# Performer attention: features by two groups of 64 contraction rows, context by swapped operands in four groups of 32 columns

## The chip, the cores and the metric

The kernel runs on one core of one Trainium2 chip. The metric is the device time of one execution in microseconds (us); lower is better. A comparison takes the median of several runs.

## The reference, cut to what matters

A batch of 8 sequences of 1024 rows by 256 columns goes through four layers: causal attention, a 4-bit-quantised MLP, Performer attention with an MLP, and a dequantised MLP. The change touches the third alone, and of it the attention:

```
q, k, v = split(video @ W.T + b)                  # 16 heads of 16 columns
def features(x, is_query):                        # proj is 64 x 16
    xp   = (x * 16**-0.25) @ proj.T               # 64 features for each head and row
    diag = sum(x**2) * 0.5 * 16**-0.5
    stab = max(xp over features)      if is_query # per row and head
           max(xp over features, rows) otherwise  # per head
    return 64**-0.5 * (exp(xp - diag - stab) + 1e-4)
qp, kp = features(q, True), features(k, False)
ctx = kp.T @ v                                    # per head 64 x 16, and kp.T @ 1 for the denominator
out = (qp @ ctx) / (qp @ sum(kp))
attn = out @ Wo.T + bo
```

## The kernel before, in words

Everything is float32 in memory. A product that needs full precision at high speed is written as three matmuls of split operands (`product`, lines 267 to 271): high part times high part, high times low, low times high. Other matmuls (transposes, context, output, half squares) take float32 operands as they are.

The Performer attention (`performer_attention`, from line 1072) works batch by batch on 8 tiles of 128 rows. For each batch there is a *front* (normalised rows are transposed, `t`; k is projected, `k`; v is projected, `v`; half squares of k, `s`; features of k for the 8 tiles, `f`), a *tail* (q is projected, the maximum over k is spread, then for the 8 tiles the features of q, the exponentials, the transposes of q's features and the context), and an *out* part (output product, division, transposes and the Wo product for the 8 tiles). `merged(b, b + 1)` interleaves the out part of one batch with the front of the next, in nine slots by the hand-written list `FRONT`; `tail(b)` runs between. All engines follow the same order, each with its own instruction list, and semaphores tie them.

- `features(i)` (line 1486): for tile i and each half c of the 256 columns of q or k, one `product` with a stationary operand of 128 rows by 128 columns (the transposed q or k) and 512 moving columns. The moving operand `proj` is block-diagonal: 8 heads of 16 rows, 64 columns each. So 6 matmuls of 128x512 for a call. It is called 8 times for k (in `front`, line 1525) and 8 times for q (in `tail`, line 1580).
- The q features of a tile go to VectorE (maximum, line 1377; add the half squares, line 1379; subtract, line 1383), to ScalarE (exponential, line 1463), back to TensorE (8 transposes, line 1586), and to ScalarE (copy, line 1460). The k features get their shift subtracted by GpSimd (line 1230) and their exponential from ScalarE (line 1457).
- The context (line 1599): for each tile 8 matmuls, one for two heads: stationary are 128 columns of k's exponentials, moving are 34 columns of v (16 columns and a column of ones for each head). Half of each 128x34 result belongs to no head pair and is not read. Before the first tile one matmul (line 1595) puts in the constant's share, with 272 moving columns `v_sum`.
- At the end of the tail VectorE copies the two useful halves into `ctx_pair` (line 1396), and TensorE's next output product (line 1544) waits for that.

In the tail TensorE's order for step i is: features of tile i, transposes of tile i - 2, context of tile i - 1. It has 10 steps.

Of the kernel before, what the change touches and what calls it, by code (L numbers as in the profile page):

```python
# [1040 lines left out]

class PerformerRaw:
# [29 lines left out]
def performer_attention(core, dram, attn_dram, raw, mlp_raw):  # L1072
# [7 lines left out]
    with ExitStack() as ctx:  # L1080
# [17 lines left out]
        with ExitStack() as prep:  # L1098
# [3 lines left out]
            @block.gpsimd  # L1102
            def _(pool):
                pool.memset(keps[:, :], KEPS).then_inc(made, 1)
                pool.memset(ones[:, :], 1.0).then_inc(made, 1)

                pool.memset(square_sum[:, :, :], 0.0).then_inc(made, 1)
                pool.wait_ge(made, 3)
                for c in range(KD):
                    pool.memset(square_sum[:, c, c * HC:(c + 1) * HC], 0.5 * DH ** -0.5).then_inc(made, 1)  # L1110
                pool.wait_ge(made, 3 + KD)
                for c in range(KD):
                    part_c = square_sum[:, c, c * HC:(c + 1) * HC]
                    pool.affine_select(out=part_c, in_=part_c, compare_op=ALU.is_ge, fill=0.0, base=0,
                                       pattern=[[-DH, HC]], channel_multiplier=1).then_inc(made, 1)
                    pool.wait_ge(made, 4 + KD + 2 * c)
                    pool.affine_select(out=part_c, in_=part_c, compare_op=ALU.is_ge, fill=0.0, base=DH - 1,
                                       pattern=[[DH, HC]], channel_multiplier=-1).then_inc(made, 1)
                pool.wait_ge(made, 3 + 3 * KD)
# [30 lines left out]
        v_sum = sbuf("p_v_sum", [P, HEADS * VW])  # L1150
# [10 lines left out]
        qfT = kf[:, :, :].rearrange("p t (k q) -> p t k q", k=PAIRS)  # L1161
        ctx_pair = sbuf("p_ctx_pair", [P, PAIRS, 2 * VW])
# [25 lines left out]
        ctx_done, ctx_copied = sem("p_ctx_done"), sem("p_ctx_copied")  # L1188
# [22 lines left out]
        @block.gpsimd  # L1211
        def _(pool):
            def tile_of_v(i):
                return v[:, i].rearrange("p h w -> p (h w)")

            with pool.Fori(0, B) as b:
                pool.wait_ge(var_ready, b + 1)
                pool.tensor_tensor(rstd[:, bass.ds(b * TB, TB)], var_eps[:, :], core.minus_half[:, :],
                                   ALU.pow).then_inc(rstd_ready, 1)
                pool.wait_ge(v_ready, b * 4 + 4)  # L1220
                for i in range(1, TB):
                    if i > 1:
                        pool.wait_ge(v_summed, b * (TB - 1) + i - 1)
                    pool.tensor_tensor(v_sum[:, :], v_sum[:, :] if i > 1 else tile_of_v(0), tile_of_v(i),
                                       ALU.add).then_inc(v_summed, 1)
# [34 lines left out]
        def _(dve):  # L1260
# [87 lines left out]
            def tail(b, last):  # L1348
# [44 lines left out]
                dve.wait_ge(ctx_done, b + 1)  # L1393
                for r in range(2):
                    rows = slice(r * M, (r + 1) * M)
                    dve.tensor_copy(ctx_pair[rows, :, r * VW:(r + 1) * VW],
                                    ps_a[rows, 0:PAIRS * 2 * VW].rearrange("p (k w) -> p k w", k=PAIRS)
                                    [:, :, r * VW:(r + 1) * VW]).then_inc(ctx_copied, 1)
# [69 lines left out]
        def _(pe):  # L1468
# [7 lines left out]

            def half_squares(b, ps, k, half):
# [80 lines left out]
            def tail(b, last):  # L1558
# [15 lines left out]
                for i in range(TB + 2):  # L1574
# [13 lines left out]
                    if 1 <= i <= TB:  # L1588
# [15 lines left out]

            pe.wait_ge(ones_set, 2)
            run(tail, merged)(pe)
# [517 lines left out]
def host_layout(inputs):  # L2124
# [11 lines left out]
    for n in "qkvo":  # L2136
        a[f"p_w{n}T"] = inputs[f"L1_attn_W{n}"].T
    for n in "kq":
        a[f"p_b{n}"] = columns(inputs[f"L1_attn_b{n}"])
# [43 lines left out]
```

## Time and profile before

| | |
|---|---|
| time, median of 3 runs | 2728.48 us (2715.63 to 2732.13) |
| the profiled execution's own time | 2712.57 us |
| its span, first to last instruction | 2710.9 us |
| mean granted TensorE clock | 0.952 |
| TensorE matmuls busy | 2439.4 us (90%), 16012 records |
| VectorE, ScalarE, GpSimd busy | 1960.4, 1196.5, 733.1 us |

The span is the time of one execution between its first and last instruction on the engines. Busy time of TensorE counts a matmul from its start to its modelled end, and neighbours overlap, so the distance from start to start is read rather than the duration. A granted clock of 1.00 is 2.4 GHz, 0.50 is 1.2 GHz.

### The profile page before, as it was taken

What the parts mean: (1) busy time and instruction counts of PE and PEld (TensorE: products, weight loads), DVE (VectorE), ACT (ScalarE), POOL (GpSimd) and SP (SyncE); (2) the same over time, 40 slices, a digit from 0 to 9 for tenths busy, and PEclk for the clock granted to TensorE, in tenths of its full rate; (3) what the DMA queues carried; (4) which work ended last, traced back from release to release, by engine and by line L of the source; (5) the groups of instructions that cost most, each with busy time, mean ns of one, the idle gap of its engine ahead of it and who ended that gap; (6) DMA issues with size and microseconds to landing.
All of it is one profiled execution on the core that took longest, in us unless ns stands there. A gap on an engine that the chain in (4) does not pass through costs nothing. (4 is left out here: it accounts for less than half of the span.)

```text
span 2710.9 us, 44219 instructions
## 1 busy us (share of the span) xinstructions
PE 2439.4 (90%) x16012; PEld 2226.7 (82%) x16012; DVE 1960.4 (72%) x3617; ACT 1196.5 (44%) x1864; POOL 733.1 (27%) x452
## 2 busy tenths in 40 slices
PE   7999996889998969999999999958888888799999
PEld 6888885888888868898898899847777777699998
DVE  5666675899999966566566656648999998866664
ACT  4444543343344325445456445523333333444444
POOL 1111111444444433123212312214344442211110
PEclk9999998899999989999999999968999989899999
DMA  5000000000000000000000000020000010100000
GB/s 168 0 0 0 0 0 19 1 1 0 0 0 0 1 16 1 16 8 8 15 12 4 15 15 8 9 67 24 17 24 15 15 39 1 41 17 23 23 23 32
DMA packets 43114, 45.94 MB, mean 17 GB/s; under 512 B 2976, under 2 KB 42016, under 8 KB 42784
## 3 DMA queue, kind: packets, MB, share of 16 engines
q1 hardware_dynamic: 43040, 44.95, 5.3%
q8 instruction: 47, 0.77, 0.1%
q14 instruction: 27, 0.22, 0.0%
HBM read 28.16 MB, written 16.78 MB: 17 GB/s over the span
## 5 line engine op out<-in xcount | busy, mean ns | idle before, releaser
L1738 ACT ACTIVATE m_a<-m_ps_wide,m_b 128x512 f32<-128x512 f32 x128 | 88.4, 691 | 286.4 <-PE m_ps_wide L271 198.6
L1706 PE MATMUL m_ps_z<-m_w_hi,m_a_hi 128*128 128x256 f32 x512 | 152.5, 298 | 53.9 <-DVE m_a_lo L1778 53.8
L1738 ACT ACTIVATE d_a<-d_ps_wide,d_b 128x512 f32<-128x512 f32 x128 | 88.3, 690 | 190.4 <-PE d_ps_wide L271 188.4
L1778 DVE TENSOR_TENSOR d_a_lo<-d_a,d_a_hi 128x512 fp32r<-128x512 f32 x128 | 86.8, 690 | 110.7 <-ACT d_a_hi L1742 109.7
L1230 POOL TENSOR_TENSOR p_kf<-p_kf,p_k_shift 128x1024 f32<-128x1024 f32 x64 | 119.4, 1903 | 155.5 <-DVE p_k_shift L1364 155.5
L1706 PEld LDWEIGHTS m_ps_z<-m_w_hi,m_a_hi 128*128 128x128 f32 x512 | 102.4, 200 | 68.6 <-DVE m_a_lo L1778 63.5
L1706 PE MATMUL m_ps_z<-m_w_lo,m_a_hi 128*128 128x256 f32 x512 | 149.5, 292 | 0.0
L1706 PE MATMUL m_ps_z<-m_w_hi,m_a_lo 128*128 128x256 f32 x512 | 149.2, 291 | 0.0
L1706 PE MATMUL d_ps_z<-d_w_hi,d_a_lo 128*128 128x256 f32 x512 | 145.4, 284 | 0.0
L1706 PE MATMUL d_ps_z<-d_w_lo,d_a_hi 128*128 128x256 f32 x512 | 145.0, 283 | 0.0
L1706 PE MATMUL d_ps_z<-d_w_hi,d_a_hi 128*128 128x256 f32 x512 | 143.9, 281 | 0.3 <-DVE d_a_lo L1778 0.3
L269 PE MATMUL f_ps_gate<-f_gate_w_hi,f_n_T_hi 128*128 128x352 f32 x256 | 93.6, 366 | 39.6 <-ACT f_silu L942 39.6
L1313 DVE TENSOR_REDUCE p_kmax<-p_kf 128x16 f32<-128x1024 f32 x64 | 78.1, 1220 | 65.4 <-ACT p_kf L1429 65.0
L194 POOL TENSOR_TENSOR f_h_q<-f_h_q,f_h_scale 128x1408 f32<-128x1408 f32 x32 | 83.2, 2599 | 155.5 <-DVE f_h_q L191 155.5
L1544 PE MATMUL p_ps_a<-p_ctx_pair,p_kf 128*128 128x34 f32 x1024 | 123.6, 277 | 0.0
L1544 PEld LDWEIGHTS p_ps_a<-p_ctx_pair,p_kf 128*128 128x128 f32 x1024 | 122.7, 196 | 0.4
L1599 PEld LDWEIGHTS p_ps_a<-p_v,p_kf 128*128 128x128 f32 x1024 | 120.2, 192 | 0.8
L1599 PE MATMUL p_ps_a<-p_v,p_kf 128*128 128x34 f32 x1024 | 119.8, 272 | 0.0
L269 PE MATMUL m_ps_wide<-m_h_hi,m_w_hi 128*128 128x512 f32 x256 | 109.0, 426 | 3.8 <-DVE m_h_lo L1771 3.7
L1937 DVE SCALAR_TENSOR_TENSOR m_o<-m_o,m_o_mean,m_g 128x256 f32<-128x256 f32 x64 | 111.9, 1807 | 0.0
L269 PE MATMUL p_ps_feat<-p_proj_hi,p_kqT_hi 128*128 128x512 f32 x256 | 111.7, 436 | 0.0
L1463 ACT ACTIVATE raw_weights<-raw_weights 128x1024 f32<-128x1024 f32 x64 | 67.8, 1060 | 98.5 <-DVE raw_weights L1383 98.5
(342 smaller groups left out, 8707.9 us busy)
## 6 DMA issues: line engine op xcount, KB each, us to landing
residual<-in_x SPq DMA_DIRECT2D x8, 1024.0 KB, 11.8
attn<-p_attn SPq DMA_DIRECT2D x32, 256.0 KB, 2.1
m_attn<-attn SPq DMA_DIRECT2D x16, 512.0 KB, 3.8
out<-residual SPq DMA_DIRECT2D x16, 512.0 KB, 2.9
raw_weights<-in_d_q SPq DMA_DIRECT2D x2, 1024.0 KB, 7.2
d_scale<-in_d_scale SPq DMA_DIRECT2D x2, 1024.0 KB, 6.0
raw_weights<-in_m_w1T SPq DMA_DIRECT2D x1, 1024.0 KB, 4.9
raw_weights<-in_m_w2T SPq DMA_DIRECT2D x1, 1024.0 KB, 9.4
```

What stands on the lines that cost most here:

```text
L194: return pool.tensor_tensor(self.blocked(v), self.blocked(v), self.spread(self.scale[slot][:, :]), ALU.mult)
L269: pe.matmul(out, lhsT[0], rhs[0], start=start, stop=False)
L1230: pool.tensor_tensor(f, f, k_shift[:, i, :].unsqueeze(2).broadcast_to([P, HEADS, M]), ALU.subtract).then_inc(k_shifted, 1)
L1313: small_k.add(dve.tensor_reduce(kmax[:, m, :], kf[:, m, :].rearrange("p (h m) -> p h m", h=HEADS), AX.X, ALU.max))
L1463: act.activation(qf[i % 2][:, :], qf[i % 2][:, :], ACT.Exp).then_inc(q_exp, 1)
L1544: mm = pe.matmul(ps_a[:, k * 2 * VW:(k + 1) * 2 * VW], qfT[:, i, k, :], ctx_pair[:, k, :], start=True, stop=True)
L1599: mm = pe.matmul(ps_a[:, k * 2 * VW:(k + 1) * 2 * VW], kf[:, j, k * P:(k + 1) * P], vt[:, k * 2 * VW:(k + 1) * 2 * VW], start=False, stop= ...
L1706: mm = pe.matmul(z, a, w[:, f, :], start=(f == 0 and k == 0 and j % 2 == 0), stop=(f == FC - 1 and k == 2), skip_group_check=True)
L1738: act.activation(self.a[f % RING][:, :], self.ps_wide[f % 2][:, :], self.func, bias=self.b1[:, f:f + 1])
L1778: dve.tensor_tensor(self.a2[1][:, f, :], self.a[f % RING][:, :], self.a2[0][:, f, :].bitcast(F32), ALU.subtract).then_inc(self.a_lo, 1)
L1937: o_tally.add(dve.scalar_tensor_tensor(o[:, j, :], o[:, j, :], o_moments.mean[:, j:j + 1], g3[:, :], ALU.subtract, ALU.mult))
```

## The change

Features: q and k are laid out so that each half c of their transposed tile holds four heads in rows 0 to 63 and four in rows 64 to 127. Each of the 6 matmuls of 128 rows by 512 columns becomes two of 64 rows by 256 columns, on the two row halves, issued next to each other and written to two different PSUM banks. A call issues 12 matmuls in place of 6. The host permutes the rows of Wq, Wk and their biases; the mask of the half squares follows.

Context: the operands are swapped. For each head a stationary operand of 17 columns (v and the ones) and 64 moving columns (k's exponentials) give a 17x64 result; the four heads issued next to each other go to PSUM partitions 0, 32, 64 and 96. So 16 matmuls for a tile in place of 8, and 16 for the constant's share in place of 1. The result is the transposed context, so at the end of the tail VectorE copies it to SBUF (128x256, over the free `squares` tile), TensorE transposes it with two 128x128 transposes, and VectorE copies the useful halves into `ctx_pair` as before. One matmul at the start of the layer fills the bank, so that rows that no head writes hold numbers.

```diff
             def features(i):
+                hi, lo = kqT
+                n = HR * M
                 for c in range(KD):
-                    mm = product(pe, ps_feat[i % 2][:, c * BANK:(c + 1) * BANK],
-                                 part(kqT, slice(None), c, slice(i * P, (i + 1) * P)), part(proj, slice(None)))
+                    for k, (a, w) in enumerate(((hi, proj[0]), (hi, proj[1]), (lo, proj[0]))):
+                        for r in range(GROUPS):
+                            rows, at = slice(r * RG, (r + 1) * RG), r * BANK + c * n
+                            mm = pe.matmul(ps_feat[i % 2][:, at:at + n], a[rows, c, i * P:(i + 1) * P],
+                                           w[rows, r * n:(r + 1) * n], start=(k == 0), stop=(k == 2))
                 return mm
...
+            def column_order():
+                return [HC * c + 2 * j + r for c in range(KD) for r in range(2) for j in range(CT)]
+
+            def ctx_at(h):
+                j, at = h % HC // 2, (h // HC * 2 + h % 2) * M
+                return ps_a[j * VP:j * VP + VW, at:at + M]
...
-                            pe.matmul(ps_a[:, 0:HEADS * VW], keps[:, :], v_sum[:, :], start=True, stop=False,
-                                      skip_group_check=True)
-                        vt = v[:, j].rearrange("p h w -> p (h w)")
-                        for k in range(PAIRS):
-                            mm = pe.matmul(ps_a[:, k * 2 * VW:(k + 1) * 2 * VW], kf[:, j, k * P:(k + 1) * P],
-                                           vt[:, k * 2 * VW:(k + 1) * 2 * VW], start=False, stop=(j == TB - 1),
-                                           skip_group_check=True)
+                            for h in column_order():
+                                pe.matmul(ctx_at(h), v_sum[:, h, :], keps[:, 0:M], start=(h < HC and h % 2 == 0), stop=False,
+                                          skip_group_check=True)
+                        for h in column_order():
+                            mm = pe.matmul(ctx_at(h), v[:, j, h, :], kf[:, j, h * M:(h + 1) * M], start=False,
+                                           stop=(j == TB - 1), skip_group_check=True)
                         if j == TB - 1:
                             mm.then_inc(ctx_done, 1)
+                pe.wait_ge(ctxT_copied, b + 1)
+                for c in range(KD):
+                    mm = pe.transpose(ps_b[:, c * P:(c + 1) * P], ctxT[:, c * P:(c + 1) * P], ident[:, :])
+                mm.then_inc(ctx_turned, 1)
...
                 dve.wait_ge(ctx_done, b + 1)
+                dve.tensor_copy(ctxT[:, :], ps_a[:, 0:KD * P]).then_inc(ctxT_copied, 1)
+                dve.wait_ge(ctx_turned, b + 1)
```

`RG = 64`, `GROUPS = 2`, `HR = 4`, `VP = 32`, `CT = 4`, `KD = 2`, `M = 64`, `VW = 17`.

## Rows read from the trace of the kernel before

**Rows 1.** Busy time by stretch (PE, PEld, DVE, ACT, POOL, then clock): tail, merged, tail's start.

```profile
1149.50:1189.00 39.50, 38.64 (x277) 35.34 (x276) 30.91 (x52) 24.03 (x25) 16.54 (x9) 0.96 0.00 0
1189.00:1240.00 51.00, 49.91 (x364) 45.93 (x363) 24.08 (x45) 20.55 (x36) 5.35 (x7) 1.00 0.06 21
...
1246.00:1257.00 11.00, 11.00 (x67) 9.84 (x66) 5.29 (x7) 2.57 (x5) 10.87 (x6) 0.84 0.00 0
```

**Rows 2.** Timeline, GpSimd, k's shift in two batches: start us, us, engine, line.

```profile
1149.46 14.92 POOL L1230 TENSOR_TENSOR p_kf<-p_kf,p_k_shift 128x1024 f32<-128x1024 f32 x8 [20.59 <-DVE p_k_shift L1364]
...
1246.13 14.92 POOL L1230 TENSOR_TENSOR p_kf<-p_kf,p_k_shift 128x1024 f32<-128x1024 f32 x8 [20.59 <-DVE p_k_shift L1364]
```

**Rows 3.** Timeline, TensorE: the tail's first feature matmul; one of its 8 steps.

```profile
1153.77 0.48 PE L269 MATMUL p_ps_feat<-p_proj_hi,p_kqT_hi 128*128 128x512 f32 x1
...
1173.56 0.48 PE L269 MATMUL p_ps_feat<-p_proj_hi,p_kqT_hi 128*128 128x512 f32 x1
1173.88 0.39 PE L270 MATMUL p_ps_feat<-p_proj_lo,p_kqT_hi 128*128 128x512 f32 x1
1174.11 0.39 PE L271 MATMUL p_ps_feat<-p_proj_hi,p_kqT_lo 128*128 128x512 f32 x1
...
1175.03 1.03 PE L1586 MATMUL p_ps_turn<-ident,raw_weights 128*128 128x128 f32 x8
1175.90 1.87 PE L1599 MATMUL p_ps_a<-p_v,p_kf 128*128 128x34 f32 x16
1177.61 0.48 PE L269 MATMUL p_ps_feat<-p_proj_hi,p_kqT_hi 128*128 128x512 f32 x1
```

**Rows 4.** Timeline, VectorE in the same tail: first steps, then waits for TensorE.

```profile
1157.10 1.74 DVE L1379 TENSOR_TENSOR p_q_shift<-p_q_shift,p_halfsq_q 128x16 f32<-128x16 f32 x1
...
1161.91 0.65 DVE L1379 TENSOR_TENSOR p_q_shift<-p_q_shift,p_halfsq_q 128x16 f32<-128x16 f32 x1
...
1165.63 0.17 DVE L1379 TENSOR_TENSOR p_q_shift<-p_q_shift,p_halfsq_q 128x16 f32<-128x16 f32 x1
1165.84 1.22 DVE L1383 TENSOR_TENSOR raw_weights<-p_ps_feat,p_q_shift 128x1024 f32<-128x1024 f32 x1
...
1175.23 1.23 DVE L1377 TENSOR_REDUCE p_q_shift<-p_ps_feat 128x16 f32<-128x1024 f32 x1 [0.55 <-PE p_ps_feat L271]
...
1179.28 1.22 DVE L1377 TENSOR_REDUCE p_q_shift<-p_ps_feat 128x16 f32<-128x1024 f32 x1 [0.39 <-PE p_ps_feat L271]
```

**Rows 5.** Timeline, end of the tail and first output product, three engines.

```profile
1186.05 1.06 ACT L1463 ACTIVATE raw_weights<-raw_weights 128x1024 f32<-128x1024 f32 x1 [0.83 <-DVE raw_weights L1383]
...
1188.32 1.07 PE L1586 MATMUL p_ps_turn<-ident,raw_weights 128*128 128x128 f32 x8
1188.52 0.62 DVE L1396 COPY p_ctx_pair<-p_ps_a 64x136 f32<-64x136 f32 x2 [1.86 <-PE p_ps_a L1599]
...
1189.22 1.95 PE L1544 MATMUL p_ps_a<-p_ctx_pair,p_kf 128*128 128x34 f32 x16
...
1191.50 0.42 DVE L1324 TENSOR_TENSOR p_mixed<-p_ps_a,p_inv_den 128x256 f32<-128x256 f32 x1
```

**Rows 6.** Timeline, TensorE in the merged stretch: v's projection (256 columns), a transpose pair.

```profile
1206.70 0.28 PE L270 MATMUL p_ps_feat<-p_wv_lo,p_nT_hi 128*128 128x256 f32 x1
1206.81 0.28 PE L271 MATMUL p_ps_feat<-p_wv_hi,p_nT_lo 128*128 128x256 f32 x1
...
1228.10 0.38 PE L1537 MATMUL p_ps_b<-ident,p_mixed 128*128 128x128 f32 x2
```

**Rows 7.** Timeline, the merged stretch's last slot: the wait there.

```profile
1236.44 0.38 PE L269 MATMUL p_ps_b<-p_wo_hi,p_mixedT_hi 128*128 128x256 f32 x1 [1.09 <-DVE p_mixedT_lo L1337]
```

**Rows 8.** Tile view of `p_ps_a`: two records for each float32 matmul; durations min/median/max in ns.

```profile
L1595 PE MATMUL p_ps_a<-p_v_sum,p_keps x16: 390/392/655, 1062.5 to 1732.8; 128*128 128x272 f32 x16
```

**Rows 9.** Timeline, weight loads: one of 16 columns, and the load after it.

```profile
1243.04 0.09 PEld L1565 LDWEIGHTS p_ps_b<-ident,p_kmax_all 128*16 128x16 f32 x1 [0.47 <-issue]
...
1243.15 0.19 PEld L269 LDWEIGHTS p_ps_feat<-p_nT_hi,p_wq_hi 128*128 128x128 f32 x1
```

More of the change, by code:

```diff
@@ L1039 @@
 HC = HEADS // KD
+RG = 64
+GROUPS, HR = P // RG, RG // DH
+VP = 32
+CT = P // VP
 class PerformerRaw:
@@ L1149, in performer_attention @@
         v = sbuf("p_v", [P, TB, HEADS, VW])
[L1150 removed]
+        v_sum = sbuf("p_v_sum", [P, HEADS, VW])
         halfsq_k, halfsq_q = (sbuf(f"p_halfsq_{e}", [P, TB, HEADS]) for e in "kq")
@@ L1161, in performer_attention @@
         qfT = kf[:, :, :].rearrange("p t (k q) -> p t k q", k=PAIRS)
+        ctxT = squares[:, 0, 0, 0:KD * P]
         ctx_pair = sbuf("p_ctx_pair", [P, PAIRS, 2 * VW])
@@ L1187, in performer_attention @@
         k_shifted, k_exp = sem("p_k_shifted"), sem("p_k_exp")
-        ctx_done, ctx_copied = sem("p_ctx_done"), sem("p_ctx_copied")
+        ctx_done, ctxT_copied = sem("p_ctx_done"), sem("p_ctxT_copied")
+        ctx_turned, ctx_copied = sem("p_ctx_turned"), sem("p_ctx_copied")
         qf_done, q_shifted, q_exp = sem("p_qf_done"), sem("p_q_shifted"), sem("p_q_exp")
@@ L1213, in tile_of_v @@
             def tile_of_v(i):
-                return v[:, i].rearrange("p h w -> p (h w)")
+                return v[:, i, :, :]
             with pool.Fori(0, B) as b:
@@ L1223, in _ @@
                         pool.wait_ge(v_summed, b * (TB - 1) + i - 1)
-                    pool.tensor_tensor(v_sum[:, :], v_sum[:, :] if i > 1 else tile_of_v(0), tile_of_v(i),
-                                       ALU.add).then_inc(v_summed, 1)
+                    so_far = v_sum[:, :, :]
+                    pool.tensor_tensor(so_far, so_far if i > 1 else tile_of_v(0), tile_of_v(i), ALU.add).then_inc(v_summed, 1)
                 pool.wait_ge(k_shift_ready, b + 1)
@@ L1396, in tail @@
                     dve.tensor_copy(ctx_pair[rows, :, r * VW:(r + 1) * VW],
-                                    ps_a[rows, 0:PAIRS * 2 * VW].rearrange("p (k w) -> p k w", k=PAIRS)
-                                    [:, :, r * VW:(r + 1) * VW]).then_inc(ctx_copied, 1)
+                                    ps_b[rows, 0:KD * P].rearrange("p (k w) -> p k w", k=PAIRS)
+                                    [:, :, 0:VW]).then_inc(ctx_copied, 1)
             dve.memset(v[:, :, :, DH:VW], 1.0).then_inc(ones_set, 1)
@@ L1594, in tail @@
                             pe.wait_ge(v_summed, (b + 1) * (TB - 1))
-                            pe.matmul(ps_a[:, 0:HEADS * VW], keps[:, :], v_sum[:, :], start=True, stop=False,
-                                      skip_group_check=True)
-                        vt = v[:, j].rearrange("p h w -> p (h w)")
-                        for k in range(PAIRS):
-                            mm = pe.matmul(ps_a[:, k * 2 * VW:(k + 1) * 2 * VW], kf[:, j, k * P:(k + 1) * P],
-                                           vt[:, k * 2 * VW:(k + 1) * 2 * VW], start=False, stop=(j == TB - 1),
-                                           skip_group_check=True)
+                            for h in column_order():
[4 more added lines that the diff above has]
+                                           stop=(j == TB - 1), skip_group_check=True)
                         if j == TB - 1:
                             mm.then_inc(ctx_done, 1)
+                pe.wait_ge(ctxT_copied, b + 1)
+                for c in range(KD):
+                    mm = pe.transpose(ps_b[:, c * P:(c + 1) * P], ctxT[:, c * P:(c + 1) * P], ident[:, :])
+                mm.then_inc(ctx_turned, 1)
             pe.wait_ge(ones_set, 2)
+            pe.matmul(ps_a[:, 0:PAIRS * 2 * VW], ident[:, :], ctx_pair[:, :, :].rearrange("p k w -> p (k w)"),
+                      start=True, stop=True)
             run(tail, merged)(pe)
@@ L2135, in host_layout, with by_row_group @@
         a[f"f_{n}"] = inputs[f"L0_ffn_w_{n}"]
-    for n in "qkvo":
+    def by_row_group(v):
+        return v.reshape(GROUPS, KD, HR * DH, -1).transpose(1, 0, 2, 3).reshape(v.shape)
+    for n in "vo":
         a[f"p_w{n}T"] = inputs[f"L1_attn_W{n}"].T
     for n in "kq":
-        a[f"p_b{n}"] = columns(inputs[f"L1_attn_b{n}"])
+        a[f"p_w{n}T"] = by_row_group(inputs[f"L1_attn_W{n}"]).T
+        a[f"p_b{n}"] = columns(by_row_group(inputs[f"L1_attn_b{n}"]))
     a["p_bv"] = inputs["L1_attn_bv"]
```

13 lines of the change are left out of this document (7 added, 6 removed).

## The prediction

> **What bounds the kernel now.** I read busy time by stretch first. In a merged stretch TensorE is busy 49.9 of 51 us and VectorE 24.1; in a tail TensorE 38.6 of 39.5, VectorE 30.9, ScalarE 24.0 [rows 1]. The reader should see TensorE full in both and VectorE as the next engine in the tail alone. Two successive batches start k's shift at 1149.46 and 1246.13 [rows 2]: a batch lasts 96.67 us, eight take about 773 us of the 2710.9. What one batch gains or loses counts eight times.
>
> The timeline gives TensorE's work from start to start. A step of the tail is 4.05 us (1173.56 to 1177.61): features 1.47 (six matmuls 0.23 apart, the first 0.32 before the second), transposes 0.87, context 1.71 [rows 3]. In the merged stretch a feature call that follows a like product takes 6 x 0.23 = 1.38. Then VectorE in the same tail: it waits for the features in the later steps, but only 0.55 and 0.39 us (a second 0.39 follows, alike) [rows 4]. So of a step of 4.05 us VectorE itself fills about 3.66 where it also normalises the next batch. Behind TensorE stands an engine that is nearly as slow.
>
> **The change part by part.**
>
> *Features.* Each matmul of 512 columns becomes two of 256 on different rows. 256 columns of this type go out 0.11 to 0.12 apart, take 0.118 [rows 6]. If the two row halves run side by side, six pairs take 6 x 0.118 = 0.71; if they run one after the other, 12 x 0.118 = 1.42, no gain on 1.38. No row of before shows two row groups at work, so these are the two ends. I take side by side, because the two touch neither the same rows nor the same bank and are issued next to each other; the nearest row, though, is the serial one. To the 0.71 I add 0.1 for the first load in front of each call (the 0.32 less 0.23 in [rows 3]) and 0.1 for going back to full height: 0.91 us. A call saves 0.47 in the merged stretch.
>
> The Trainium skill ("TensorE: Matmul & The Clock Gate", Part 3, on packing small matmuls) measured 3.07 times for four row groups of 32, an efficiency of 77%; as an estimate, two groups would then give 1.54 times and a call would be about 1.1 us in place of 0.91. No run here shows it yet.
>
> *k's features in the merged stretch.* TensorE is full there, so a shorter call moves what follows. Five calls lie in slots 5 to 7: 5 x 0.47 = 2.35. In the last slot are three. There TensorE already stands 1.09 us for VectorE's low half of the mixed tile [rows 7]; what f5 saves is added to that wait. Behind it ScalarE's copies and VectorE's maxima follow each other with 1.2 us each, so of the three calls about 0.9 us arrive. Together 3.25, less some 0.15 for new short waits of the same kind in slots 6 and 7: **3.1 us a batch**.
>
> *Context.* A float32 matmul leaves two records (16 for 8 matmuls), and 272 columns last 392 ns, as long as 512 columns of the features [rows 8, 3]: each column costs about two. So 64 columns are like 128; by the line through 0.118 at 256 and 0.23 at 512, one record is 0.0625 us. Now a tile has 16 records at 1.71 / 16 = 0.107, whatever its 34 columns. After, 32 records. Ends: all apart at today's 0.107, 3.42 us; streamed one after another at 0.0625, 2.0; neighbouring heads side by side in different columns, half of that, 1.0. I take 1.5, between the last two: loads of 17 columns are short (0.09 against 0.19 for 128 [rows 9]), but the two records of a head share their columns and can't overlap. The constant's share becomes 16 matmuls too: 1.5 for 0.46 before. It lies in the step in which TensorE waits for VectorE's first subtraction, and the earlier features leave room for it; without that room it costs 1.0 us.
>
> *A step of the tail* is then 0.91 + 0.87 + 1.5 = 3.3 us on TensorE. VectorE needs about 3.66 where it normalises (above) and, by its share of 30.9 us in a whole tail, some 3.3 elsewhere; ScalarE less [rows 1]. So the tail becomes VectorE's, and what it gains is read from VectorE's chain:
> - The first features end earlier: six at 0.23 and more (the clock is at 0.84 here [rows 1]) against pairs, about 0.8 us. VectorE's little addition (line 1379) takes 1.74 and 0.65 us in the first two steps, 0.17 later [rows 4]; each time it ends at a boundary of GpSimd's 1.87 us instructions (14.92 / 8 from 1149.46 [rows 2]: 1158.8, 1162.5). Start 0.8 earlier and the first ends one boundary sooner, at 1156.9, the second at 1160.7, and the third at 1164.4, when GpSimd is done. The third subtraction then starts at 1164.4 instead of 1165.84: 1.5 us gained.
> - The waits for features go: 0.55 + 0.39 + 0.39 = 1.33 us.
> - The last exponential ended at 1187.1, yet the last transposes began at 1188.32, since the context of the last tile stood in front [rows 5]. Now that context is done before: 1.2 us.
> - Added: the turn. Today's copies (0.62) lie under the last transposes [rows 5]. After, VectorE's 128x256 copy (0.42, as line 1324 [rows 5]) is hidden there too, but the two transposes (0.38 [rows 6]) and the copies (0.62) stand in front of the first output product: with hand-overs 1.2 us. Nothing else is queued on VectorE behind this wait but the first division, which needs that product anyhow.
>
> Tail: 1.5 + 1.33 + 1.2 - 1.2, about **2.8 us a batch**. The single matmul at the start, the masks and the host's permutation cost nothing that shows.
>
> *Sum.* 3.1 + 2.8 = 5.9, times 8 = 47 us: from 2712.57 to 2665.4 for an execution like the profiled one. That one lies 16 us under the median of the runs; for the median I take the same difference: 2728.5 - 47 = **2681 us**, 1.7% less.
>
> **The rivals.**
>
> *Each change of shape costs.* The matmul's duration beyond its distance, 0.39 - 0.23 = 0.16 us [rows 3], is what stands if the array must run empty between full height, half height and narrow columns. Three changes in a step of the tail: 0.81 + 0.87 + 1.5 + 0.48 = 3.66, still about VectorE's; in the merged stretch two for a call, so a call saves 1.38 - 0.71 - 0.32 = 0.35, 8 calls some 2.2. With 2.3 left of the tail 4.5 us a batch, 36 in all: 2692. Against a cost at all: the load after the narrow one of 16 columns started 0.11 us behind it, before that matmul had ended [rows 9]. The Trainium skill ("TensorEngine Tiling (Array Packing)", Key Properties) says that changing the tiling mode drains the engine; this is its rule.
>
> *The row halves don't overlap* (the change doesn't do what it says). A call is 1.42 + 0.2. Merged: 8 x 0.24 = 1.9 us worse. A step of the tail is 1.62 + 0.87 + 1.5 = 4.0, as now, and 1.0 of the constant's share shows, against a shorter start of the context: about nothing. Sum +1 to +2 us a batch: 2728 + 12 = 2740; 2770 if the columns don't overlap either. For it: no row shows a distance between load-and-matmul pairs under 0.107.
>
> *The narrow context matmuls go out no faster than today's pairs.* This is the one on the slower side. The tail's TensorE work is 8 x 0.91 + 8 x 0.87 + 1.2 + 9 x 32 x p = 15.4 + 288p, p the time of one record; from the first features to the first output product are now 35.45 us (1153.77 to 1189.22 [rows 3, 5]). With p = 0.107: 46.2, 10.8 worse, less 3.1: +7.7 a batch, +61: 2790, 2.2% slower. It decides from 15.4 + 288p = 35.45 + 3.1, p = 0.080: above that the change loses. For it: 0.107 is the distance of the context's, the outputs' and the transposes' records alike. Against: all of these load 128 columns, and these load 17; if the load sets the distance, it falls.
>
> *The clock falls in the tail.* It is at 0.84 where the half squares' narrow matmuls have run [rows 1], against 1.00 in the merged stretch. If the narrow context does the same to every step and the clock falls to half, features and transposes double, 0.91 + 0.87 more: a step near 5.1 us, over 1 us above now, some +60 us.
>
> **How the numbers follow.** Forecast (both groups overlap enough) 0.45; cost of changing shape 0.15; row halves don't overlap 0.18; context at p above 0.080 0.15; clock 0.05; something else 0.02. About 1%, 27 us, is what a measurement of this kernel can tell from no change. Faster by over 1%: the first two, 0.60. Within 1%: the third with the rest, 0.19. Slower: 0.21. The best case is no extra cost of a call (8 x 0.67 = 5.4 merged) and one boundary of GpSimd more in the tail (4.9): 10.3 x 8 = 82, 2646. The low end is 2642. The high end takes in the row halves that don't overlap and p a little above its turning point: 2752. The forecast's own range is 2650 to 2700.
>
> **What the new profile would show.** A feature call under 1.0 us from start to start, its pairs about 0.12 apart, says the row groups overlap; 1.4 says they don't. Context of a tile: 1.5 if right, 2.0 if streams are serial, 3.4 if pairs are. VectorE's waits for features gone in the tail, and the small addition ending a boundary earlier. Distance between two batches' shifts near 90.8. The first output product some 1.2 us after the last transposes. Wrong it would be by a gap at each change of shape, by a lower clock in the tail, or by new waits in slots 6 to 8 that eat more than 0.15 us.

## The result and the profile after

| | before | after |
|---|---|---|
| time, median | 2726.95 us (2715.63 to 2732.13) | 2772.18 us (2763.19 to 2781.4) |
| ratio, 95% interval | | 1.0176 (1.0137 to 1.0214) |
| the profiled execution, its span | 2712.57, 2710.9 us | 2763.19, 2761.5 us |
| mean granted TensorE clock | 0.952 | 0.915 |
| TensorE matmuls busy | 2439.4 us, 16012 records | 2397.3 us, 18062 records |

A median here takes in every run of a kernel and a ratio only those within 1.5% of its fastest, so a ratio need not be the quotient of two medians: features alone below has a median of 2859.9 us with its slow run and of 2852.6 us without.

TensorE is busy 42 us less and the kernel is 1.8% slower. The two new matmul forms are as fast as forecast or faster. TensorE's timeline, a merged slot and a step of the tail (compare [rows 3]):

```profile
1219.48 0.39 PE L1516 MATMUL p_ps_feat<-p_proj_hi,p_kqT_hi 64*128 64x256 f32 x2
1219.71 0.28 PE L1516 MATMUL p_ps_feat<-p_proj_lo,p_kqT_hi 64*128 64x256 f32 x2
1219.83 0.28 PE L1516 MATMUL p_ps_feat<-p_proj_hi,p_kqT_lo 64*128 64x256 f32 x2
...
1220.18 0.28 PE L1516 MATMUL p_ps_feat<-p_proj_hi,p_kqT_lo 64*128 64x256 f32 x2
1220.39 0.44 PE L1565 MATMUL p_ps_b<-ident,p_mixed 128*128 128x128 f32 x2
...
1173.58 0.64 PE L1627 MATMUL p_ps_a<-p_kf,p_v 128*17 128x64 f32 x32
1174.15 0.39 PE L1516 MATMUL p_ps_feat<-p_proj_hi,p_kqT_hi 64*128 64x256 f32 x2
...
1175.83 1.07 PE L1614 MATMUL p_ps_turn<-ident,raw_weights 128*128 128x128 f32 x8 [0.70 <-ACT p_kf L1475]
```

Pairs of 64-row matmuls are 0.12 us apart and a call takes 1220.39 - 1219.48 = 0.91 us, in place of 1.38. The 32 records of a tile's context take 1174.15 - 1173.58 = 0.57 us, in place of 1.71. The transposes now wait for ScalarE: TensorE is no longer what a step of the tail lasts by.

The loss stands elsewhere. TensorE's loop body is one batch, so the program jumps back six times. At each jump, between the last features of k (the end of a merged stretch) and the first projection of q (which opens the tail), TensorE's timeline has a hole:

```profile
1233.87 0.58 PE L1516 MATMUL p_ps_feat<-p_proj_hi,p_kqT_hi 64*128 64x256 f32 x2
...
1236.38 0.41 PE L1516 MATMUL p_ps_feat<-p_proj_hi,p_kqT_lo 64*128 64x256 f32 x2
1241.66 0.58 PE L269 MATMUL p_ps_feat<-p_nT_hi,p_wq_hi 128*128 128x512 f32 x1 [4.87 <-issue]
1242.05 0.63 PE L270 MATMUL p_ps_feat<-p_nT_lo,p_wq_hi 128*128 128x512 f32 x1
```

"issue" means that the engine waited for nothing that the profile shows. The waits of TensorE over the eight batches (what waited, for whom, us in total, times, longest):

```profile
PE p_ps_turn L1614 <- ACT p_kf L1475: 48.9, 44, 2.1
PE p_ps_feat L269 <- issue: 33.8, 6, 6.2
```

The instruction queue of the whole page (packets, MB, share):

```profile
q8 instruction: 111, 1.82, 0.3%
```

and in the DMA view of 1230 to 1245 us alone:

```profile
q8 instruction: 3, 0.05, 1.6%
```

Six jumps, six holes, 4.9 to 6.2 us each, 33.8 us in all. The queue that brings instructions moved 111 packets; on the page of before it is 47 packets and 0.77 MB. Three of them fall in the 15 us around this jump.

The clock is the other change. Windows at the end of the next batch's tail (columns as in [rows 1]):

```profile
1276.00:1280.00 4.00, 3.13 (x59) 2.53 (x56) 3.93 (x8) 3.34 (x4) 0.00 (x0) 1.00 0.02 4
1280.00:1284.00 4.00, 2.06 (x72) 1.75 (x72) 3.63 (x7) 3.34 (x4) 0.00 (x0) 1.00 0.00 0
1284.00:1288.00 4.00, 2.29 (x33) 1.92 (x21) 1.02 (x3) 2.09 (x3) 0.00 (x0) 0.99 0.02 4
1288.00:1292.00 4.00, 4.00 (x21) 4.00 (x20) 0.88 (x3) 0.60 (x1) 0.00 (x0) 0.50 0.00 0
1292.00:1296.00 4.00, 4.00 (x21) 4.00 (x21) 1.78 (x4) 0.87 (x2) 0.00 (x0) 0.50 0.00 0
```

TensorE is busy 2.06 and 2.29 of 4 us in the last steps of the tail, and then the clock is 0.50, 1.2 GHz, while it is busy all the time. Over 1050 to 1850 us the granted clock is 0.85 after and 0.95 before.

The pace of the batches separates two stretches: from the start of k's shift to the first output product (the tail), and from there to the next shift (the merged stretch, the jump and q's projections). All following numbers of this kind are such distances, read from GpSimd's and TensorE's timeline; means over the batches of one execution:

| | tail, us | rest, us |
|---|---|---|
| before | 39.2 (37.9 to 40.3) | 56.8 |
| after | 38.1 | 64.0 |
| loop written out | 38.1 | 58.6 |
| written out and filled | 38.1 (37.4 or 38.8) | 54.0 |
| context alone, written out and filled | 38.6 | 56.8 |

The tail gained 1.1 us of the forecast 2.8, and the rest, forecast to be 3.1 shorter, is 7.2 longer.

### The profile page after: what moved, and what is told of

Its sections match the earlier page's. It is cut to its first block and busy times, and to the rows that moved or that the text cites. A ratio compares the mean times of both kernels' runs of the same rounds, so it can differ in the third digit from the quotient of the medians.

```text
span 2761.5 us, 48326 instructions
## 1 busy us (share of the span) xinstructions
PE 2397.3 (87%) x18062; PEld 2181.7 (79%) x18062; DVE 1964.8 (71%) x3625; ACT 1193.7 (43%) x1864; POOL 732.9 (27%) x452
## 3 DMA queue, kind: packets, MB, share of 16 engines
q8 instruction: 111, 1.82, 0.3%
## 5 line engine op out<-in xcount | busy, mean ns | idle before, releaser
L1572 PEld LDWEIGHTS p_ps_a<-p_ctx_pair,p_kf 128*128 128x128 f32 x1024 | 141.7, 221 | 7.6 <-DVE p_ctx_pair L1411 7.6
L1572 PE MATMUL p_ps_a<-p_ctx_pair,p_kf 128*128 128x34 f32 x1024 | 142.2, 300 | 5.7 <-DVE p_ctx_pair L1411 5.7
L269 PE MATMUL f_ps_gate<-f_gate_w_hi,f_n_T_hi 128*128 128x352 f32 x256 | 93.0, 363 | 39.8 <-ACT f_silu L942 39.8
L1614 PE MATMUL p_ps_turn<-ident,raw_weights 128*128 128x128 f32 x512 | 81.6, 311 | 49.5 <-ACT p_kf L1475 48.9
L1302 DVE SCALAR_TENSOR_TENSOR p_kqT_lo<-p_ps_feat,raw_weights,p_kqT_hi 128x512 fp32r<-128x512 f32 x64 | 48.1, 751 | 107.4 <-ACT p_squares L1431 107.4
L1614 PEld LDWEIGHTS p_ps_turn<-ident,raw_weights 128*128 128x128 f32 x512 | 65.6, 160 | 60.5 <-issue 57.3
L269 PE MATMUL m_ps_wide<-m_h_hi,m_w_hi 128*128 128x512 f32 x256 | 109.4, 427 | 3.7 <-DVE m_h_lo L1805 3.7
L178 POOL TENSOR_TENSOR f_h_q<-f_h_q,f_h_inv 128x1408 f32<-128x1408 f32 x32 | 83.1, 2597 | 103.1 <-DVEq L898 103.1
```

The costliest lines, as they stand in the source:

```text
L178: return pool.tensor_tensor(self.blocked(v), self.blocked(v), self.spread(self.inv[slot][:, :]), ALU.mult)
L269: pe.matmul(out, lhsT[0], rhs[0], start=start, stop=False)
L1572: mm = pe.matmul(ps_a[:, k * 2 * VW:(k + 1) * 2 * VW], qfT[:, i, k, :], ctx_pair[:, k, :], start=True, stop=True)
L1614: mm = pe.transpose(ps_turn[:, k * P:(k + 1) * P], qf[i % 2][:, k * P:(k + 1) * P], ident[:, :])
```

## The experiments

Each time below is a median; "before" was run again beside each group of experiments (2720.95, 2728.49, 2719.15 and 2723.8 us), and a ratio is to the one beside it. These medians of one and the same kernel lie up to 10 us apart, so differences between kernels of different groups are given by the ratios too, where it matters.

**The loop written out, after and before.** TensorE's loop over batches becomes straight code; the other engines keep theirs.

```diff
-                with eng.Fori(0, B - 1) as b:
+                for b in range(B - 1):
                     tail(b, False)
                     merged(b, b + 1)
```

> The changed kernel with TensorE's loop over the batches written out (no jump back; all other engines keep their loops). Theory F (fetch): at each of the 6 jumps back TensorE waits about 5 us for its instructions, because the body has grown from 1318 to 1830 loads and matmuls; written out, the gap goes and with it the cold clock behind it: 2680 to 2700 us, instruction traffic still high but ahead of need. Rival C (clock and waits): the gap is the smaller part, TensorE's clock falls since it waits for ScalarE and VectorE in the tail: about 2735 us with the clock still near 0.92.

> The kernel before with TensorE's loop written out. F: the body of before was not fetched anew, so nothing is won: 2727 us within 0.5%. If this too falls by 1% or more, the loop cost something before as well, and F is incomplete.

The changed kernel came to 2715.74 us (ratio 0.9969, 0.9949 to 0.999), between the two expectations: 56 us less. The holes are gone: "issue" no longer stands among the waits before L269. The wait for ScalarE stayed (49.0 us, 43 times), and so did the clock of 0.85. The kernel before came to 2726.28 us (1.0025, 1.0 to 1.0049): its jump costs nothing. So the hole belongs to the changed program, and with it gone 35 to 40 us of the gap to the forecast remain. The two profiled executions of the changed kernel, with the loop and without, differ by 39.8 us, for holes of 33.8; each is at the near end of its runs, and what makes up the other 16 us between the medians was not read from a trace.

**One part alone, with the loop.** Features by row groups with the old context (the change's hunks on the masks, `features` and the host's permutation); then the new context with the old features (the others). The lines that differ most:

```diff
 features alone
+                            mm = pe.matmul(ps_feat[i % 2][:, at:at + n], a[rows, c, i * P:(i + 1) * P], ...
 context alone
+                            mm = pe.matmul(ctx_at(h), v[:, j, h, :], kf[:, j, h * M:(h + 1) * M], start=False, ...
```

> Only the features by two row groups, context as before, with the loop. Body 1510 loads and matmuls. F: if that still fits, no gap and about 3 us a batch won in the merged stretch, 2700 us; if not, the gap of 5 us six times, 2730. Rival D (the gap belongs to tiled matmuls before the jump, whatever the size) expects the gap here for sure, 2730. C: no gap needed, clock as before, 2700.

> Only the context by swapped operands, features as before, with the loop. Body 1638. F: gap if the limit lies below 1638: tail gain about 3 us a batch less 5 us six times, 2730; else 2705. D expects no gap (the matmuls before the jump are of full height), 2705. C expects the low clock in the tail here, 2740.

Features alone: 2859.88 us (1.0465, 1.0389 to 1.054), far worse than both parts together and than the 2730 expected at most. Context alone: 2755.48 us (1.0122, 1.0078 to 1.0166), expected at 2705 to 2740. Neither part is the good one; both lose, and their losses don't add. Features alone stands 34.2 us at "issue" at its six jumps (19.3 before a first matmul of a product, 14.9 before a third). Context alone, with the longer body, stands only 1.6 to 1.7 us at three jumps, which the profile puts down to ScalarE, and 0.5 us at a fourth.

**Many instructions or row groups?** In the kernel before, each feature matmul of 512 columns is split in two of 256 at full height: the same work, with as many loads and matmuls in the loop (1510, counted in the program) as the features-only kernel. Before has 1318, context alone 1638, after 1830.

```diff
...
+                        for u in range(2):
+                            mm = pe.matmul(ps_feat[i % 2][:, c * BANK + u * w:c * BANK + (u + 1) * w],
+                                           a[:, c, i * P:(i + 1) * P], m[:, u * w:(u + 1) * w],
...
```

> The kernel before, with each feature matmul of 512 columns split in two of 256 at full height: the same work, no row groups, and as many loads and matmuls in TensorE's loop as the features-only kernel has (1510 against 1318 of before). Theory 'size of the loop': the body is fetched anew at each jump back; the instruction queue moves about 100 packets in place of 47 and a gap of 1.5 to 5 us stands at the first projection after the jump, 6 times, so 2730 to 2755 (some 0.02 us more for each feature call beside). Rival 'row groups before the jump, whatever the size': 47 packets, no gap, 2721 to 2728.

It came to 2768.16 us (1.0146, 1.0101 to 1.0191), 13 us beyond the expected range, for no change of shape at all. TensorE's timeline at one jump, and the instruction queue of the page:

```profile
1148.45 0.49 PE L269 MATMUL p_ps_feat<-p_nT_hi,p_wq_hi 128*128 128x512 f32 x1 [1.78 <-ACT p_kf L1429]
1148.78 0.40 PE L270 MATMUL p_ps_feat<-p_nT_lo,p_wq_hi 128*128 128x512 f32 x1
1151.61 0.80 PE L271 MATMUL p_ps_feat<-p_nT_hi,p_wq_lo 128*128 128x512 f32 x1 [2.43 <-issue]
1152.20 0.63 PE L269 MATMUL p_ps_feat<-p_nT_hi,p_wq_hi 128*128 128x512 f32 x1
```

```profile
q8 instruction: 102, 1.67, 0.3%
```

The hole is there in two pieces. The second falls between matmuls of one product, which no semaphore parts: the instructions themselves were missing. Behind it the matmuls soon stand 0.43 us apart: the clock is at half. The rival (row groups, whatever the size) is refuted: without any row group the queue moves as many packets as with features alone, and TensorE stands 26.5 us at six jumps (18.9 at "issue", 7.6 put down to ScalarE). No run had this kernel written out, so how much of its 40 us is the hole and what is cold behind it was not measured apart.

The size of the body decides whether it is fetched again, but not alone how long TensorE stands. Context alone has more instructions than this kernel and stands far less. Ahead of its jump lie feature matmuls of 512 columns, half as many instructions for the same time. That this is the reason is an argument; no run tested it.

The packets say what is fetched. One is 1.82 MB / 111 = 16.4 KB. Written out, before moves 78 against 47, 31 packets for six more copies of the body: a loop body that stayed at hand moves nothing when it is run again. The changed kernel moves 94 written out and 111 as a loop, features alone 84 and 102: such a body is fetched anew in every round, as in straight code, and 17 or 18 packets more, about 3 for each of six jumps (context alone, 88 and 94, only 1, and its hole was the small one). Straight code pays no hole for the same packets. That the surplus is code beyond the jump, read ahead and thrown away while the loop's start is missing, fits this but was not seen by itself.

The Trainium skill ("Advanced Engine Details and Errata", ISA Cache) gives TensorE 128 KB in lines of 16 KB, 256 instructions each. The packets agree: 16.4 KB each, and 31 for six copies of 1318 loads and matmuls are about 255 a packet. By 128 KB, as an estimate 2048 instructions, all these loops would stay at hand, up to the 1830 loads and matmuls of after; by its "Only 2 cache lines" not even 1318 would. Here one of 1318 stays and one of 1510 doesn't, and the measurement decides.

**The clock, causally.** Written out, and matmuls of 512 columns, whose result nobody reads, are put where TensorE would wait for ScalarE.

```diff
+                fill = {5: 2, 6: 3, 7: 3, 8: 7, 9: 3, 10: 3}
+                def idle_matmuls(i, out):
+                    for _ in range(fill.get(i, 0)):
+                        pe.matmul(out, kqT[0][:, 0, 0:P], kqT[0][:, 0, 0:BANK], start=True, stop=True)
...
+                        if i == 2:
+                            pe.wait_ge(k_shift_ready, b + 1)
+                        idle_matmuls(i, ps_b[:, :])
                         pe.wait_ge(q_exp, b * TB + i - 1)
...
+                idle_matmuls(TB + 2, ps_feat[0][:, 0:BANK])
```

The added wait makes sure that VectorE has read `ps_b` before the idle matmuls write it.

> The changed kernel with TensorE's loop written out (as in the run that came to 2715.7) and, in the later steps of the tail, matmuls of 512 columns whose result nobody reads, put where TensorE would stand and wait for ScalarE: 2, 3, 3, 7 and 3 of them before the transposes of tiles 3 to 7, and 3 before the first output product. They cost 0.22 us each and all lie in waits. Clock theory: what is left missing is the granted clock that falls to half when TensorE stands in steps 8 and 9, and stays there for the turn and the first two output products (3.47 us for 16 products that take 1.9 at full clock). Kept busy, the clock stays at 1.0 there: 3 to 4 us a batch come back, 2685 to 2695, and mean clock in the batches 0.9 or more in place of 0.85. Rival (the chain through ScalarE and VectorE is what lasts, the clock costs nothing): 2716 or some us more.

It came to 2693.02 us (0.9883, 0.9844 to 0.9922), in the expected range: 23 us won by adding work, and faster than before by 1.2%. The granted clock over 1050 to 1850 us is 0.91 in place of 0.85. The end of its tail, windows and TensorE:

```profile
1266.00:1270.00 4.00, 3.88 (x53) 2.69 (x51) 1.38 (x5) 2.75 (x3) 0.00 (x0) 1.00 0.02 4
1270.00:1274.00 4.00, 4.00 (x37) 3.86 (x37) 1.71 (x4) 1.36 (x3) 0.00 (x0) 1.00 0.00 0
```

```profile
1263.23 1.88 PE L1617 MATMUL p_ps_b<-p_kqT_hi 128*128 128x512 f32 x7
...
1272.92 1.87 PE L1583 MATMUL p_ps_a<-p_ctx_pair,p_kf 128*128 128x34 f32 x16
```

The first output product of a batch, which took 3.47 us at half clock in the written-out kernel, takes 1.87. The tail is no shorter for it (38.1); what falls is the rest, 58.6 to 54.0, because the merged stretch begins at full clock and there TensorE is the bound.

> The changed kernel with its loop, and with the fill-in matmuls of the run that came to 2693.0 (loads and matmuls in the loop 1914 in place of 1830). If the jump and the clock are two separate costs that add: the fill-in gives back the 23 us that it gave without the loop, 2772 - 23 = 2749, and the gaps of 4.9 us at the jump stand as before. If the fill-in matmuls, being long, keep TensorE at work while the loop's first instructions come, they'd have to lie before the jump; they lie in the tail, so the gaps should not shrink.

With the loop and the fill-in: 2740.98 us (1.0085, 1.0058 to 1.0113); 33.1 us at "issue" in six holes, as in the changed kernel. The two costs stand side by side: by medians the fill-in gives 31 us with the loop and 23 without, writing out 56 without the fill-in and 48 with it; by the ratios, each to its own before, 25 and 23, 56 and 55. They add.

**More fill-in, in the first steps.**

```diff
-                fill = {5: 2, 6: 3, 7: 3, 8: 7, 9: 3, 10: 3}
+                fill = {2: 6, 3: 5, 4: 2, 5: 2, 6: 3, 7: 3, 8: 7, 9: 3, 10: 3}
...
```

> The unrolled and filled kernel (2693.0) with more matmuls that nobody reads, now also in the first steps of the tail, where TensorE stands 1.76 and 1.75 us and the clock is at 0.81, 0.76 or 0.60, 0.83, 0.74 in three stretches of 4 us: 6 before q's third features, 5 before the transposes of tile 1, 2 before those of tile 2. Clock theory: the cold stretch of the first steps goes, a batch like that from 1139.65 to 1232.45 (92.8 us) becomes one of 91.4 or a little less: 1 to 1.5 us a batch, 2681 to 2687. Rival (the first steps go by VectorE's and GpSimd's chain, so their clock costs nothing): 2693, within 3 us.

2697.04 us (0.9916, 0.9889 to 0.9944; five rounds). Nothing won: its tails still take 37.4 or 38.8, the last one 36.4. The clock theory's condition was met in part only: beside the last tail two of the others have no cold stretch. These two last 37.4 us, and so does one with a cold stretch, so the rival holds for the tail. But behind each of the two the rest lasts 57.0 us in place of 54.0. Windows and TensorE in the first of them:

```profile
1206.00:1213.00 7.00, 7.00 (x67) 6.84 (x66) 2.16 (x6) 1.25 (x3) 3.05 (x5) 1.00 0.01 2
1213.00:1219.80 6.80, 6.80 (x41) 6.14 (x40) 3.45 (x5) 1.88 (x4) 2.26 (x3) 0.50 0.00 0
```

```profile
1209.38 1.85 PE L1516 MATMUL p_ps_a<-p_square_sum,p_squares 128*128 128x16 f32 x16
...
1212.33 2.89 PE L1583 MATMUL p_ps_a<-p_ctx_pair,p_kf 128*128 128x34 f32 x16
...
1219.54 0.40 PE L1527 MATMUL p_ps_feat<-p_proj_hi,p_kqT_lo 64*128 64x256 f32 x2
```

The clock fell with TensorE busy all the time before, on 16-column half squares, 64-row features and 34-column products, and it was back 6.8 us later, with no matmul of 512 columns between. So an idle TensorE is not the only thing that stands ahead of a fall; what moved it here stays open.

**Each part written out, and context filled.** The edits are those above, put together; for the last one:

```diff
+                fill = {7: 1, 8: 7, 9: 3, 10: 3}
...
```

> Features by row groups alone, with TensorE's loop written out. This takes the jump's part out of the 2859.9 us of the kernel with the loop. If only the jump had been wrong: 6 gaps of 5.3 us are 32, with the cold stretch behind each perhaps 60, so 2800 from 2860. If the clock that falls at the start of the tail and then stays at half for up to 60 us is a matter of its own: still 2790 or more. If the fall of the clock was itself started by the gap at the jump: all of it goes, about 2690 (half of the forecast gain).

> Context by swapped operands alone, with TensorE's loop written out. With the loop it was 2755.5, with gaps of 1.7 us at the jump. The gaps gone are 10 us, with what is cold behind them 15 to 30: 2725 to 2745. By step times of the tail it should be faster than before (context of a tile 0.57 in place of 1.71 us), so if it is not under 2720, the clock at the end of the tail and the turn eat what the context gives.

> Context by swapped operands alone, loop written out (2755.4), with the same kind of matmuls that nobody reads: 1, 7 and 3 before the transposes of tiles 5, 6 and 7, where TensorE stood up to 1.92 us, and 3 before the first output product. What the swapped context gives when neither the jump nor the clock stands against it: in the run without them the cold stretch at the end of the tail was some 12 us long in each batch, and half of that is lost, so 4 to 5 us a batch, 2715 to 2725; the rest up to 2693 (22 to 32 us) is then what the row-group features give under the same conditions. If the turn and the tail's chain ate the context's gain by themselves, it stays at 2750.

Features alone, written out: 2813.37 us (1.032, 1.0279 to 1.0361). 47 us went with the jump, the rest is clock. Windows of its profile, and TensorE where the clock returns:

```profile
1143.00:1147.00 4.00, 4.00 (x34) 3.91 (x32) 1.18 (x2) 2.21 (x3) 4.00 (x3) 0.94 0.00 0
1147.00:1213.00 66.00, 66.00 (x347) 63.74 (x347) 33.35 (x58) 25.24 (x28) 12.20 (x7) 0.50 0.00 1
1214.80:1230.00 15.20, 15.20 (x113) 14.17 (x112) 6.84 (x15) 6.53 (x13) 0.00 (x0) 1.00 0.06 18
```

```profile
1213.93 0.63 PE L270 MATMUL p_ps_feat<-p_nT_lo,p_wk_hi 128*128 128x512 f32 x1
1214.36 0.59 PE L271 MATMUL p_ps_feat<-p_nT_hi,p_wk_lo 128*128 128x512 f32 x1
1214.78 0.40 PE L269 MATMUL p_ps_feat<-p_nT_hi,p_wk_hi 128*128 128x512 f32 x1
```

66 us at 1.2 GHz with TensorE busy in every one of them. Ahead of it stand the half squares (32 records of 16 columns); in it 64-row features, transposes and 34-column products; at its end come the Wo product of 256 columns and, at 1213.36, the first full-height matmuls of 512 columns. Five of eight tails last 54 us or more, and the others 36 to 39. But the next tail of the same execution starts on the same kinds of matmul and is cold for 3.4 us alone:

```profile
1269.40:1272.80 3.40, 3.40 (x27) 2.94 (x24) 2.28 (x4) 0.00 (x0) 3.40 (x3) 0.50 0.00 0
1272.80:1277.00 4.20, 4.20 (x43) 4.03 (x42) 4.13 (x6) 2.01 (x2) 4.20 (x3) 1.00 0.02 4
```

So these matmuls don't hold the clock down by their kind alone.

Context alone, written out: 2755.43 us (1.0111, 1.0071 to 1.0151), as with the loop; the expectation of 2725 to 2745 was wrong, its small hole cost nothing that shows. Filled: 2718.77 us (0.9978, 0.996 to 0.9997), 37 us less and in the expected range. So what the context alone lost was the clock at the end of its tail, and with that held it is worth about 5 us. The step to both parts, 2718.8 to 2693.0, is the features' share: 26 us.

**Waking the clock.** Features alone, written out, with 8 full-height matmuls of 512 columns, read by nobody, between q's half squares and q's features.

```diff
                     half_squares(b, ps_a, 1, half)
+                pe.wait_ge(k_shift_ready, b + 1)
+                for _ in range(8):
+                    pe.matmul(ps_b[:, :], kqT[0][:, 0, 0:P], kqT[0][:, 0, 0:BANK], start=True, stop=True)
```

> Features by row groups alone, loop written out (2813.4), with 8 full-height matmuls of 512 columns, whose result nobody reads, between q's half squares and q's features. In the run without them the clock was at 0.50 from the half squares to the first projections of the next merged stretch, 66 us, in which TensorE never stood but had no full-height matmul of 512 columns. Theory (the half squares leave the clock at half, and the 64-row features, transposes and 34-column products don't bring it back, while full-height ones do): the clock returns behind these 8; they cost 1.9 to 3.4 us a batch, 15 to 27 in all, and the cold tails go (about 20 us each in half of the batches, 90 in all): 2725 to 2750. Rival (the clock is low for another reason in every other batch, or 64-row features bring it down again): 2813 to 2840.

2786.65 us (1.0206, 1.015 to 1.0262), between the two expectations: neither holds as it stood. Windows at one batch's matmuls, behind them, and later:

```profile
1251.00:1255.00 4.00, 4.00 (x14) 3.06 (x15) 0.29 (x1) 0.00 (x0) 4.00 (x3) 0.57 0.00 0
1255.00:1264.00 9.00, 8.28 (x86) 7.62 (x88) 7.96 (x11) 2.77 (x3) 6.91 (x4) 1.00 0.01 2
1268.00:1312.00 44.00, 44.00 (x228) 42.83 (x228) 19.09 (x39) 18.08 (x20) 1.65 (x1) 0.50 0.00 1
```

```profile
1251.49 3.47 PE L1597 MATMUL p_ps_b<-p_kqT_hi 128*128 128x512 f32 x8
...
1266.29 1.06 PE L1610 MATMUL p_ps_turn<-ident,raw_weights 128*128 128x128 f32 x8 [1.85 <-ACT p_kf L1476]
1267.19 2.61 PE L1623 MATMUL p_ps_a<-p_v,p_kf 128*128 128x34 f32 x16
```

They run at half clock (3.47 us for 8) and the clock is full behind them. A wait of 1.85 us for ScalarE then precedes the next fall, and again the clock stays at half for 44 us and more. Now two of eight tails are of that kind, 56 us; the others take 41 to 44, the 8 matmuls included. So the clock came back behind that work in this batch, and in two batches it fell again in the tail. That the 8 matmuls bring the clock back fits this batch and the 27 us won, but it isn't shown: the short cold stretches above ended without any.

## Why the prediction was wrong

**The step that failed** lies in the part-by-part costing: an added instruction was priced at the time between its record and the next, and nowhere at what it does to the loop it stands in. The text forecast 32 records for 16 in each context tile and pairs for each feature matmul, yet took the loop body as free to grow. It grew from 1318 loads and matmuls to 1830, no longer stayed at hand, and TensorE stood 33.8 us at six jumps; written out, 48 to 56 us come back. None of the named rivals is this; it lay in the 0.02 of something else.

**The second step** is the clock rival at 0.05. It named the clock, but another way for it to fall: it asked whether narrow matmuls make every step of the tail cold. Instead faster matmuls left TensorE idle at the end of the tail, the clock fell there, and the bill came in the stretch behind it, where TensorE is full. 23 to 31 us by the fill-in, against "+60 or more". The same text had counted TensorE's step at 3.3 us against VectorE's 3.66 and taken the idle time as free.

**The sum without these two** is the kernel written out and filled: 2693.0 against a forecast of 2681, and against a before of 2728.5 in the same group 35 us for the 47. By the paces: tail 1.1 and rest 2.8, together 3.9 us a batch, times 8 = 31.

The two profiled executions (2712.57 and 2691.74) differ by 21 us only, and this is no fault of the paces. Behind the last tail stands an out part without a front. In before's profiled execution it lasts 35.2 us; in before written out, an execution of 2731.41 us, 47.3 us for the same work, and in all the other kernels here 45 to 49:

```profile
1763.50:1798.70 35.20, 29.50 (x194) 27.30 (x192) 8.85 (x24) 6.79 (x16) 0.00 (x0) 0.77 0.07 23
```

```profile
1769.60:1816.90 47.30, 41.59 (x194) 38.93 (x192) 8.85 (x24) 6.82 (x16) 0.00 (x0) 0.53 0.05 17
```

There TensorE's work has gaps, and the clock falls to half: 2.9 us after the start of the stretch in the one written out, 19.4 us after it in the other. It is worth 12 of the 16 us by which the prediction found its profile under the median, and the reason to set the median, not the profiled time, against the forecast. The other terms:
- *Features call 0.91 us*: 0.91. The row halves run side by side, and that rival falls. The estimate of 1.1 that the prediction worked out from the Trainium skill's packing figure ("TensorE: Matmul & The Clock Gate", Part 3) was too high.
- *k's features, 3.1 us a batch*: 2.8 to 2.9 (56.9 to 54.0). Right. With the context alone it stays at 56.9, so all of it is the features'. The last slot's wait grew from 1.09 [rows 7] to 1.43, about the third of a microsecond that the forecast gave away.
- *Context of a tile 1.5 us*: 0.57, a record each 0.018 us. The line through the feature matmuls' durations was the wrong scale for loads of 17 columns, and neighbouring heads run side by side. The rival above p = 0.080 falls. That it went below the forecast 1.5 brought nothing that shows, as TensorE waits for ScalarE in the tail either way.
- *Tail 2.8 us*: 1.1. Here the mechanism was right and its size was read from one batch, not a typical one. VectorE's small addition again ended with GpSimd's instructions, at the forecast places; its rows in the changed kernel's tail of the same batch:

```profile
1157.33 0.21 DVE L1392 TENSOR_TENSOR p_q_shift<-p_q_shift,p_halfsq_q 128x16 f32<-128x16 f32 x1
...
1160.62 0.65 DVE L1392 TENSOR_TENSOR p_q_shift<-p_q_shift,p_halfsq_q 128x16 f32<-128x16 f32 x1
...
1164.34 0.64 DVE L1392 TENSOR_TENSOR p_q_shift<-p_q_shift,p_halfsq_q 128x16 f32<-128x16 f32 x1
1165.02 1.23 DVE L1396 TENSOR_TENSOR raw_weights<-p_ps_feat,p_q_shift 128x1024 f32<-128x1024 f32 x1
```

  The third subtraction starts 14.99 us behind the shift (1150.03), forecast 14.9, before 16.38. That tail lasts 37.4 us against 39.76: 2.4, near the 2.8. But three of the eight tails of before are of a shorter kind already and lasted 37.9, and in the filled kernel four of eight are of its longer kind (38.8, the last 38.5). Short against short and long against long the gain is 0.5 to 1.0 us. The forecast took the batch of 96.67 us for all; the mean of seven is (1723.74 - 1052.26) / 7 = 95.93.
- *The turn, 1.2 us*: from the two transposes at 1186.33 to the product at 1187.43, 1.1. Right.
- *Changing shape costs*: about 0.1 us a change, already in the 0.91: the first pair of a call stands 0.23 before the second, others 0.12, and the last 0.21 before the transposes (1220.18 to 1220.39). That rival falls, and with it the drain as a price that matters here.

**Both parts hide each other's fault.** Features alone is the slowest kernel of all (2859.9). In the changed kernel, with the packed context, the tail's cold stretches end after one or two steps; with the 34-column products they last for most of the tail in five batches of eight. What exactly makes that difference stays open: no run changed the context's form and left TensorE's idle time as it was.

## What to carry to other kernels

A change that trades long matmuls for more, shorter ones is priced in instructions of the loop body too: compare the instruction queue's packets of loop and straight code, look for "issue" at the first matmul behind the jump, and write the loop out or keep the body small. When an engine whose clock falls stops being the bound in one stage, look at the stage behind it: its idle time is paid where it is the bound again, and matmuls that nobody reads can be cheaper than waiting, though more of them were not better here. Before taking a gain from one batch, list that distance for all batches; here two kinds of tail, 1.4 to 1.9 us apart, stood side by side before and after. And ask whether the profiled execution is like the median one: here one stretch at the end of the layer took 12 us less in it.

## What the runs showed of the hardware

- TensorE fetched loop bodies of 1510, 1638 and 1830 loads and matmuls anew in each round (102, 94 and 111 packets on the page; 47 for one of 1318, which was not fetched again). It stood up to 6.2 us at the jump with 1830, and at most 1.7 us with 1638.
- 64-row matmuls of split operands on different rows and banks ran in pairs, a pair of 256 columns every 0.12 us; float32 records with 17-column weights and 64 columns, neighbours in different groups of 32 columns, went out every 0.018 us. The Trainium skill ("TensorE: Matmul & The Clock Gate", "Wait — 56ns, not 53.3ns?") says that start to start never drops below about 25 ns; in four column groups it did.
- The granted clock stayed at 0.50 for 66 us in which TensorE was busy throughout, mostly with 64-row, 34-column and transpose work (features alone, written out). In the same execution it stayed there for 3.4 us alone on such work, and with more fill-in it fell to 0.50 for 6.8 us without an idle moment ahead of it.
